# A graph attention layer on one core: the prologue's normalisation, score masks and weight preparation in another order

## The reference

```
h  = max(layernorm(x), 0)
Wh = h @ W;   f1 = Wh @ a1;   f2 = Wh @ a2
e  = leaky_relu(f1[:, None] + f2[None, :], 0.2)
att = softmax(where(adj > 0, e, -9e15), axis=1)
out = x + elu(att @ Wh)
```

## Time and profile before

| what | us |
|---|---|
| median of three runs (lowest to highest) | 1041.62 (1041.38 to 1043.15) |
| the profiled execution's own time | 1041.01 |
| its span, first to last instruction | 1039.2 |
| busy: PE, DVE, ACT, POOL | 952.9, 962.6, 937.5, 487.7 |
| first make_wh starts | 15.99 |
| mask_scores(0) starts | 44.69 |

### The profile page before, as it was taken

One profiled execution on the slowest core, in us unless ns is written; L12 is line 12 of the kernel. 1 busy time (PEld: TensorE's weight loads), 2 busy tenths in 40 slices (PEclk: granted clock), 3 DMA queues, 4 the chain that ended last, 5 costly groups with the idle time before them and its releaser, 6 DMA issues. The chain is left out here.

```text
span 1039.2 us, 24022 instructions
## 1 busy us (share of the span) xinstructions
PE 952.9 (92%) x8971; PEld 827.7 (80%) x8971; DVE 962.6 (93%) x1259; ACT 937.5 (90%) x1479; POOL 487.7 (47%) x510
## 2 busy tenths in 40 slices
PE   4677999999999999999999999999999999888897
PEld 3565888888888888888888888888888888777786
DVE  5799999999999999999999999999999999999963
ACT  2599999999999999999999999999999999988873
POOL 3344333545445454454545545355454453554543
PEclk9999999999999999999999999999999999999999
DMA  8466565777767677677676767667767666757514
GB/s 233 118 182 185 162 187 162 206 202 203 198 183 208 198 200 212 179 211 201 196 205 178 215 198 204 195 182 207 204 196 208 187 191 175 199 170 200 153 52 152
DMA packets 323235, 194.82 MB, mean 187 GB/s; under 512 B 7472, under 2 KB 319024, under 8 KB 323120
## 3 DMA queue, kind: packets, MB, share of 16 engines
q1 hardware_dynamic: 323120, 193.29, 65.6%
HBM read 176.42 MB, written 16.84 MB: 186 GB/s over the span
## 5 line engine op out<-in xcount | busy, mean ns | idle before, releaser
L418 PE MATMUL acc<-v,direct 128*128 128x256 f16 x1024 | 279.3, 273 | 14.9 <-ACT z_direct L522 7.8
L654 DVE CUSTOM_DVE_ANT_0 prob<-tp,f_row 128x2048 f32<-128x2048 bf16 x128 | 291.8, 2280 | 0.0
L422 PE MATMUL acc<-v,direct 128*128 128x256 f16 x1024 | 279.1, 273 | 0.0
L420 PE MATMUL acc<-v,direct 128*128 128x256 f16 x1024 | 279.1, 273 | 0.0
L401 PE MATMUL acc_st<-v,stored 128*128 128x256 f16 x992 | 270.4, 273 | 0.0
L402 PE MATMUL acc_st<-v,stored 128*128 128x256 f16 x992 | 270.4, 273 | 0.0
L400 PE MATMUL acc_st<-v,stored 128*128 128x256 f16 x992 | 270.4, 273 | 0.0
L743 POOL TENSOR_SCALAR small_total<-total 128x1 f32<-128x1 f32 x128 | 47.7, 373 | 470.4 <-ACT prob L488 470.4
L488 ACT ACTIVATE prob<-prob,shift 128x2048 f32<-128x2048 f32 x128 | 256.5, 2004 | 10.5
L481 ACT ACTIVATE prob<-prob,f 128x2048 f32<-128x2048 f32 x128 | 255.7, 1998 | 0.0
L749 POOL TENSOR_TENSOR direct<-prob,inv 128x1024 f16<-128x1024 f32 x128 | 242.3, 1893 | 10.0
(11 more groups left out here) (81 smaller groups left out, 1263.4 us busy)
## 6 DMA issues: line engine op xcount, KB each, us to landing
raw<-in_adj SPq DMA_DIRECT2D x128, 1024.0 KB, 5.9
y<-in_x SPq DMA_DIRECT2D x64, 256.0 KB, 5.1
out<-y SPq DMA_DIRECT2D x64, 256.0 KB, 3.1
x_in<-in_x SPq DMA_DIRECT2D x108, 128.0 KB, 5.1
f_row<-f_scratch SPq DMA_DIRECT2D x31, 256.0 KB, 5.0
stored<-in_x SPq DMA_DIRECT2D x4, 512.0 KB, 7.8
f_scratch<-f_t SPq DMA_DIRECT2D x124, 0.5 KB
stored<-in_x SPq DMA_DIRECT2D x4, 128.0 KB, 2.2
```

Of the source, the lines that this page charges most:

```text
L418: nc.tensor.matmul(acc[:, m, :], p_d[:, 0, rows], v_c[:, 0, :], start=(j == 0 and m % 2 == 0), stop=False, skip_group_check=True)
L420: nc.tensor.matmul(acc[:, m, :], p_d[:, 0, rows], v_c[:, 1, :], start=False, stop=False, skip_group_check=True)
L422: last = nc.tensor.matmul(acc[:, m, :], p_d[:, 1, rows], v_c[:, 0, :], start=False, stop=(j == C - 1), skip_group_check=True)
L654: nc.vector.tensor_tensor_reduce(out=prob[:, c % 2, :], in0=tp_b, in1=f1_row[:, b % 2, :], scale=1.0, scalar=-3.0e38, op0=ALU.add, op1=ALU ...
```

## The change

`measured_at` gives a list: chunks 0 to 3 at steps -26 to -23 as before, then two chunks a step (4 to 11 at steps -22 to -19), then chunk s + 30 up to chunk 19 at step -11; from chunk 20 on it is s + 23 as before. POOL's root(g) moves to step 4g - 20, behind the normalise of the last chunk of group g - 1 (`root_at`); for groups 1 to 4 make_offset(g) moves to step 4g - 21 (`offset_at`), make_offset(0) into step -23 ahead of the weights. From group 5 on both stand where they stood. The ring of statistics (`RS`) grows from 8 to 12 chunks.

The products of W and a are made and added up in one DVE instruction each (`tensor_tensor_reduce` with an accumulator); ACT's `add_up_w` is gone. `largest_of_all` comes before them, and PE's `spread_max_w` before its first transpose of x. The DMAs of W and a are issued by ACT as its first instructions.

make_mask(0) moves to step -5 and make_mask(1) to step -2; PE's transpose_mask(0) moves ahead of make_wh(16), ACT's keep_last_f1 ahead of make_h(17), and split_v_low(16) from step -1 to step 0, behind mask_scores(0).

```diff
--- before.py
+++ after.py
@@ -40,7 +40,7 @@
     RV = 34
     RF = 20
     RX = 6
-    RS = 8
+    RS = 12
     RY = 4
     RZ = 4
     RE = 2
@@ -127,7 +127,6 @@
         w_max_one = sem("w_max_one")
         w_max_all = sem("w_max_all")
         w_scaled = sem("w_scaled")
-        w_times_a = sem("w_times_a")
         w_ready = sem("w_ready")
         f1_turned = sem("f1_turned")
         f1_spread = sem("f1_spread")
@@ -189,8 +188,24 @@
 
         def measured_at(s):
 
-            c = s + 26 if s + 26 < EARLY else s + 23
-            return c if c >= EARLY or s + 26 < EARLY else None
+            if s < -22:
+                return [s + 26]
+            if s < -18:
+                return [2 * s + 48, 2 * s + 49]
+            c = s + 30 if s + 30 < EARLY else s + 23
+            return [c] if (c >= EARLY or s + 30 < EARLY) and c <= LAST else []
+
+        def offset_at(s):
+
+            g, late = divmod(s + 21, 4)
+            if late == 0 and 1 <= g < EARLY // 4:
+                return g
+            g, late = divmod(s + 20, 4)
+            return g if late == 0 and EARLY // 4 <= g < CH // 4 else None
+
+        def root_at(s):
+            g, late = divmod(s + 20, 4)
+            return g if late == 0 and 0 <= g < CH // 4 else None
 
 
         def sent(piece):
@@ -295,9 +310,6 @@
 
             for c in range(4):
                 sp.dma_start(x_buf(c), x[0, c * P:(c + 1) * P, :]).then_inc(x_early_in[c], 16)
-            sp.dma_start(w_nat, W.rearrange("(k p) o -> p k o", p=P)).then_inc(w_in, 16)
-            sp.dma_start(a_flat,
-                         a.rearrange("o one -> one o").to_broadcast([P, 2 * FO])).then_inc(a_in, 16)
             for g in range(1, EARLY // 4):
                 r = 4 * g % C * P
                 sp.dma_start(x_early[:, 4 * g:4 * g + 4, :],
@@ -425,15 +437,14 @@
 
             pe.wait_ge(ident_f, 1)
             turn_max_w()
+            spread_max_w()
             for s in range(-18, 0):
                 transpose_x(s + LEAD + 1)
-                if s == -18:
-                    spread_max_w()
                 if s == -1:
                     spread_last_f1()
+                    transpose_mask(0)
                 if chunk(s + LEAD):
                     make_wh(s + LEAD)
-            transpose_mask(0)
             for s in range(END + 2):
                 if chunk(s + LEAD):
                     make_wh(s + LEAD)
@@ -449,13 +460,6 @@
 
         @block.scalar
         def _(act):
-            def add_up_w():
-                for i in range(4):
-                    k, side = divmod(i, 2)
-                    act.wait_ge(w_times_a, i + 1)
-                    nc.scalar.activation(w_a[:, i, :], w_a[:, i, :], ACT.Copy,
-                                         accum_out=w_cat[:, k, FO + side:FO + side + 1]).then_inc(w_ready, 1)
-
             def take_f(c):
                 act.wait_ge(wh_ps, c + 1)
                 if c // 4 == 5:
@@ -536,11 +540,12 @@
                 act.wait_ge(z_relu, k + 1)
                 nc.scalar.activation(elu[:, k % RE, :], elu[:, k % RE, :], ACT.Exp, scale=-1.0).then_inc(z_exp, 1)
 
-            add_up_w()
+            act.dma_start(w_nat, W.rearrange("(k p) o -> p k o", p=P)).then_inc(w_in, 16)
+            act.dma_start(a_flat, a.rearrange("o one -> one o").to_broadcast([P, 2 * FO])).then_inc(a_in, 16)
             for s in range(-18, 0):
-                make_h(s + LEAD + 1)
                 if s == -1:
                     keep_last_f1()
+                make_h(s + LEAD + 1)
                 if chunk(s + LEAD):
                     take_f(s + LEAD)
                     split_v_high(s + LEAD)
@@ -582,8 +587,9 @@
                 dve.wait_ge(a_in, 16)
                 for i in range(4):
                     k, side = divmod(i, 2)
-                    nc.vector.tensor_tensor(w_a[:, i, :], w_nat[:, k, :], a_row[:, side, :], ALU.mult
-                                            ).then_inc(w_times_a, 1)
+                    nc.vector.tensor_tensor_reduce(
+                        out=w_a[:, i, :], in0=w_nat[:, k, :], in1=a_row[:, side, :], scale=1.0, scalar=0.0,
+                        op0=ALU.mult, op1=ALU.add, accum_out=w_cat[:, k, FO + side:FO + side + 1]).then_inc(w_ready, 1)
 
             def largest_w():
                 dve.wait_ge(w_in, 16)
@@ -598,7 +604,7 @@
 
             def scale_w():
                 dve.wait_ge(w_max_all, 1)
-                dve.wait_ge(w_times_a, 4)
+                dve.wait_ge(w_ready, 4)
                 link(nc.vector.tensor_scalar(tops[:, 2:3], max_all, 1e-30, None, ALU.max))
                 link(nc.vector.reciprocal(tops[:, 3:4], tops[:, 2:3]))
                 nc.vector.tensor_scalar(tops[:, 4:5], tops[:, 2:3], 2.0 ** -P_BITS / W_TOP, None, ALU.mult)
@@ -626,7 +632,7 @@
 
             def add_eps(g):
                 dve.wait_ge(mv_s, 4 * g + 4)
-                wait(dve, rstd_s, g - 1)
+                wait(dve, rstd_s, g - RS // 4 + 1)
                 rs = slice(4 * g % RS, 4 * g % RS + 4)
                 nc.vector.tensor_scalar(var_eps[:, rs], mv[:, rs, 1], EPS, None, ALU.add).then_inc(var_s, 1)
 
@@ -690,33 +696,38 @@
                                                in1=h_prime(k), op0=ALU.add, op1=ALU.max).then_inc(elu_ready, 1)
 
             for s in range(FIRST, END + 2):
-                c = measured_at(s)
-                last_of_group = c is not None and chunk(c) and c % 4 == 3
                 if chunk(s):
                     mask_scores(s)
                 n = block_at(s - 1)
                 if n is not None and not first_half(n):
                     add_halves(n)
-                if c is not None and chunk(c):
+                for c in measured_at(s):
                     statistics(c)
                     aggregate(c)
-                if last_of_group:
-                    add_eps(c // 4)
+                    if c % 4 == 3:
+                        add_eps(c // 4)
                 if s == -23:
                     largest_w()
-                if chunk(s + LEAD):
+                if s == 0:
+                    split_v_low(LEAD - 1)
+                if chunk(s + LEAD) and s != -1:
                     split_v_low(s + LEAD)
                 if chunk(s + LEAD) and (s + LEAD) % 4 == 3 and sent((s + LEAD) // 4):
                     turn_f1((s + LEAD) // 4)
                 if chunk(s - 1):
                     split_low(s - 1)
-                if last_of_group:
-                    make_offset(c // 4)
+                if offset_at(s) is not None:
+                    make_offset(offset_at(s))
                 if s == -23:
+                    make_offset(0)
+                    largest_of_all()
                     multiply_w()
-                    largest_of_all()
                     scale_w()
-                if chunk(s + 2):
+                if s == -5:
+                    make_mask(0)
+                if s == -2:
+                    make_mask(1)
+                if chunk(s + 2) and s >= 0:
                     make_mask(s + 2)
                 for k in finish(s - 1):
                     finish_elu(k)
@@ -751,7 +762,7 @@
 
             def root(g):
                 pool.wait_ge(var_s, g + 1)
-                wait(pool, xn_ready, 4 * g - 4)
+                wait(pool, xn_ready, 4 * g + 4 - RS)
                 rs = slice(4 * g % RS, 4 * g % RS + 4)
                 nc.gpsimd.tensor_tensor(rstd[:, rs], var_eps[:, rs], minus_half[:], ALU.pow).then_inc(rstd_s, 1)
 
@@ -774,9 +785,8 @@
                     finish_add(k)
                 if chunk(s + LEAD + 2) and s < 0:
                     normalise(s + LEAD + 2)
-                c = measured_at(s)
-                if c is not None and chunk(c) and c % 4 == 3:
-                    root(c // 4)
+                if root_at(s) is not None:
+                    root(root_at(s))
 
 
 # ---- launch: one core; inputs and output as the reference has them ----
```

## The result

The changed kernel takes 1035.26 us, the median of 4 runs (1034.65 to 1036.42), against 1041.84 for the kernel before beside it: ratio 0.9934, with a 95% interval of 0.9921 to 0.9948. That is 6.6 us less, where 1034.0 and 7.6 less were forecast. The profiled execution took 1034.65, its span is 1032.8. A second comparison of the same two kernels, among the experiments, gave 0.9937 (0.9925 to 0.9950). The profiled execution is the fastest of the four.

A forecast was written before the change was run, and what follows sets the result against it. DVE was taken to bound the loop (busy 98.1 of 100 us), so only its start could move: 2.5 + 4.0 - 0.9 + 2.0 = 7.6 us less, median 1034.0; range 1032.5 to 1036.4 (0.70), 8 in 10 for 1031.7 to 1037.4.

The forecast's parts named there:

- The loop hands on what the prologue gains: From attention(0) to the end: the loop stays as long as now, so the prologue's 7.6 us arrives whole.
- The slower case: Rival in the loop: small_total meets DVE's mask every step; at 0.1 a step costs 12.8, giving 1046.8; chance 0.06.
- The three stalls, 4.0: Chunks 4 to 17: PE's three waits, one a group, for a group's first normalised chunk go, gaining 4.0 us.
- the slack of 0.3: Chunks 4 to 17: a group's first normalise is done at 2.9, PE wants it at 3.3, leaving 0.3 us.
- Mask 0 ahead of normalise(16), 0.9: Before chunk 16: make_mask(0) behind offset(4) holds up POOL's normalise(16), a new stall costing 0.9 us (bounds 0 and 1.2).
- The tail, 2.0: End of the prologue: attention(0) comes 5.6 us after chunk 17's transpose instead of 7.58, gaining 2.0.
- Up to chunk 4, 2.5: Start of the prologue: PE transposes chunk 4 at about 18.75 instead of 21.26, gaining 2.5 us.
- Neither moves, for W's DMA leaves earlier and the statistics ahead of it are the same: Weights at the start: DVE's largest |W| stays at 5.50 and POOL's root(0) still ends at 7.08.
- the collision with POOL: Weights: POOL's normalises of chunks 0 to 3 hold up DVE's products beside them, costing 1.0 us (0.15 to 1.8).
- The read of f1, 1.5 ahead: End of the prologue: the third quarter of f1's row lands at 35.2, 1.5 us ahead of its need at 36.7.
- It would have to double it: Read of f1: mask 2's load, issued just behind, would matter only if it doubled the read's 3.0 us.
- The clock: PE's clock, granted 0.50 from 48 to 50 around the start: nothing counted, though it can give back 0.3 us.

The follow-up runs named there:

- second pair of profiles: The kernel before and the changed kernel, each run once more unchanged as controls: 1042.90 in one run, and 1035.97, ratio 0.9937.
- Its own run: The kernel before with only the change's order of statistics, roots and offsets (ring of 12): 1035.71, ratio 0.9937.
- both edits together: The changed kernel with the DMAs of W and a issued by SP behind x, and mask 0 at step -4: 1033.39, ratio 0.9917.
- the last two runs: Both edits plus chunk 22's statistics behind mask_scores(0): 1034.33; changed kernel with SP issuing a behind x, W between x's second and third chunks: 1035.51.

## Why the prediction was right, point by point

**The loop hands on what the prologue gains**: right. From attention(0) to the end of the span the fourteen profiles have 992.2 to 993.7 us (before 992.2 and 993.5, after 992.4 and 992.6), with no order in which a kernel with the early start is longer; the two profiles of the kernel before alone lie 1.3 apart. The slower case, more meetings of small_total and mask, did not come: it took 378 ns in the mean against 373 (392 and 398 in the second pair of profiles).

**The three stalls, 4.0**: right in size. Chunk 4 to 17 took 14.93, where 14.2 + 0.9 was forecast, and the slack of 0.3 was there at chunks 8 and 12 (0.37 from the end of POOL's normalise to PE's transpose). Its own run gave the whole ratio of the change. The prediction has the stalls at the wrong chunk, though: it says that PE waits for the first chunk of a group, whose normalise waits for its offset. In the kernel before PE stood before chunks 5, 9 and 13, the second of a group, because POOL had the root of the next group to do first:

```profile
33.40 1.01 POOL L756 TENSOR_TENSOR rstd<-var_eps,minus_half 128x4 f32<-128x4 f32 x1 [2.62 <-DVE var_eps L631]
...
35.01 0.44 PE L350 MATMUL pre<-ident,stored 128*128 128x128 f32 x2 [1.20 <-POOL stored L761]
```

What the root waited for, the statistics of the next group, is as the prediction says, and so the cure is the same.

**Mask 0 ahead of normalise(16), 0.9**: right in mechanism, a little less in size: 0.7 (14.93 - 14.2), and it went when the mask was moved (14.27).

**The tail, 2.0**: 2.16, from 7.58 to 5.42, in the whole and in the masks' own run.

**Up to chunk 4, 2.5**: this term was mis-sized; it measured 1.2 (21.26 to 20.09; in the second pair of profiles 2.4, 21.57 to 19.21). Two parts of it were wrong and partly cancelled, which is luck: chunk 4's statistics were forecast at 11.55 and came at 13.00, with the products 2.6 late at their start and 1.1 of that made good. "Neither moves, for W's DMA leaves earlier and the statistics ahead of it are the same" failed: the two transfers of 256 KB, issued at 0.72 and 1.21 beside x's, made the eps 2.1 to 2.9 late. Against that, the collision with POOL cost the products nothing in these two (1.0 was counted), and they took 1.4 instead of 1.7. In other profiles (only a's DMA on SP, both edits together, and the last two runs) the first product was held for 0.1 to 0.3 and the last for 0.2, so DVE mostly goes on, and at most 0.5 was lost of the 1.0. That agrees with the Trainium skill (SBUF — State Buffer, section Who interferes with whom) in that the two exclude each other; strict turns are not what the rows show, for the four normalises were the ones that stretched.

**The read of f1, 1.5 ahead**: wrong as a margin. It took 4.1 and landed at about 37.5, 0.2 ahead of the scores at 37.76, which followed chunk 22's statistics without a wait; in the second profile it took 3.5 and was 0.8 ahead. In variants with an earlier start it did hold the scores, for 0.56, 0.69 and 1.50. "It would have to double it" was wrong: half as long again was enough there. In the changed kernel attention(0) was set by wh(17), whose f came at 40.12.

**The clock**: it fell as before, to 0.50 (the 1.2 GHz level) in 46 to 48, but later against the work: attention(1) came 6.84 after attention(0), and 7.23 before (47.02 to 54.25). That is no gain of the change. In the second profile of the same kernel the clock was at 0.50 already in 44 to 46 (0.97 in the first), and attention(1) came 7.24 after attention(0). And the 0.4 did not last in the first one either: from attention(0) to the end it has 992.4 against 992.2. Counting nothing was right.

**What is not settled**: alone, the parts give 6.6 (statistics), 2.0 (masks), about 0.2 (products) and cost 1.2 (DMAs), 7.6 in sum, and the whole gives 6.6. The mask's stall of 0.7, which the masks' own run did not have because POOL was ahead of PE there, fills most of that gap only by argument, and a gap of 1.0 is within the intervals (1.4 us to either side for the statistics alone and for the whole).

## What to carry to other kernels

Where engines stall at group boundaries on a chain of small instructions, take the chain's first links ahead of time, as many as their buffers allow: that part alone gave as much as the whole change here, whose other parts gave and cost about the same. Before a DMA is issued earlier, ask which transfer is wanted first: here 512 KB issued beside 384 KB that were wanted first cost 1.0 to 1.3 us by itself and brought nothing. And take a landing time from several executions, for here the landing of W in one profile went into forecasts that missed by 1.7 us (attention(0) with both DMAs on SP) and 1 us (the DMAs alone).

## What the runs showed of the hardware

W's DMA, issued as SP's fifth at 2.6, landed after 2.9 in one execution of the kernel before and after 4.5 in another, with nothing changed: 0.6 of those 1.6 us reached the first scores (44.69 and 45.27). A multiply with a sum over 256 elements on DVE takes 0.41, starts every 0.345 with its accumulator read, and so costs no more than the plain multiply (0.42). The read of 256 KB for f1's row took 3.0 to 3.3 with no load issued within 1.5 us behind it, and 3.5 to 4.5 in seven profiles with 1 MB issued 0.4 to 0.6 behind it; with 1.1 between them it took 3.1. The granted clock falls once to 0.50 (the 1.2 GHz level) in the loop's first steps in every profile, but not at the same place of the work: at about 45.9 in one execution of the changed kernel and at about 42.8 in another, 5.4 and 3.2 us after attention(0). In the three profiles in which it fell over 5 us after attention(0), attention(1) came 6.83 to 6.85 after attention(0), in the other eleven 7.23 to 7.24.
